# A two-layer attention and expert kernel: the first experts' second matmul as three rounded products, gates applied to finished sums, and sums and remainders moved to GpSimd

## What is computed

```python
def _L0_ffn_ref(x, Wg, W1, W2, W3):          # E=8 experts, F=256 hidden, top k=2
    scores = jnp.einsum('bsd,ed->bse', x, Wg)
    topk_scores, topk_idx = jax.lax.top_k(scores, k)
    topk_probs = jax.nn.softmax(topk_scores, axis=-1)
    h1 = jnp.einsum('bsd,efd->bsef', x, W1)
    h2 = jnp.einsum('bsd,efd->bsef', x, W2)
    hidden = jax.nn.silu(h1) * h2
    expert_out = jnp.einsum('bsef,edf->bsed', hidden, W3)
    onehot = jax.nn.one_hot(topk_idx, scores.shape[-1], dtype=x.dtype)
    gating = jnp.einsum('bsk,bske->bse', topk_probs, onehot)
    return jnp.einsum('bse,bsed->bsd', gating, expert_out)
```

## Time and profile before

| | |
|---|---|
| time, median of 3 runs | 1642.62 us |
| time of the profiled execution | 1642.04 us |
| its span | 1639.9 us |
| TensorE busy | 1490.6 us (91%) |
| VectorE busy | 1375.4 us (84%) |
| ScalarE busy | 1146.4 us (70%) |
| GpSimd busy | 167.9 us (10%) |

### The profile page before, as it was taken

How to read it: one execution, slowest core, us unless ns; L and a number is a source line. 1 busy time by engine, 2 the same in 40 slices (tenths; PEclk the granted TensorE clock), 3 DMA queues, 4 the chain that set the end, 5 groups by cost and what they waited for, 6 DMA issues and landing times.

```text
span 1639.9 us, 31494 instructions
## 1 busy us (share of the span) xinstructions
PE 1490.6 (91%) x11072; PEld 766.9 (47%) x11072; DVE 1375.4 (84%) x2375; ACT 1146.4 (70%) x1781; POOL 167.9 (10%) x231
## 2 busy tenths in 40 slices
PE   7998989599999999969999999999999998988996
PEld 4333333266556566623333333333333335766774
DVE  4899999668878678778999999999999963778776
ACT  4999999433332233217999999999999986766664
POOL 0000000101101001010000000000000001333332
PEclk9999999799999999967999999999999997999999
DMA  6635422221134322111111111111111111112111
GB/s 195 204 116 166 128 90 84 98 69 59 51 101 125 125 84 86 65 39 58 38 36 48 43 42 36 36 36 36 36 42 36 36 31 47 53 57 74 48 54 40
DMA packets 71022, 116.72 MB, mean 71 GB/s; under 512 B 23808, under 2 KB 33920, under 8 KB 70272
## 3 DMA queue, kind: packets, MB, share of 16 engines
q1 hardware_dynamic: 70912, 115.21, 23.1%
HBM read 73.49 MB, written 41.16 MB: 70 GB/s over the span
## 4 chain that ended last, share of the span: by engine, by line
PE 47%; DVE 21%; issue 12%; ACT 12%; DMA 4%; POOL 2%; SPq 2%; DVEq 0%; ACTq 0%; POOLq 0%
PE full_o L712 12%; PE max_pair L683 9%; ACT cprobs L485 7%; DVE negmax_h L801 7%; PE hid_pair L1021 7%; PE score L697 3%; PE causal_o L457 3%; PE bank L1114 3%; PE bank L1126 2%; DVE hid L1427 2%; PE triple L441 2%; DVE lin_u L1423 2%; DMA k_scr<-qk_hi 1%; DMA o_rcp<-rcp_scr 1%; SPq L960 1%
## 5 line engine op out<-in xcount | busy, mean ns | idle before, releaser
L765 ACT ACTIVATE probs<-score 128x512 f32<-128x512 f32 x1024 | 546.7, 597 | 84.3 <-PE score L697 64.3
L801 DVE TENSOR_REDUCE negmax_h<-max_pair 128x2 f32<-128x1024 f32 x512 | 587.4, 1215 | 19.6 <-PE max_pair L683 19.6
L712 PE MATMUL full_o<-probs,v_st 128*32 128x256 f32 x4096 | 331.0, 396 | 17.2 <-ACT o_sb L773 17.2
L697 PE MATMUL score<-q_st,k_st 32*128 32x512 f32 x1024 | 316.3, 501 | 4.2 <-ACT probs L765 4.2
L683 PE MATMUL max_pair<-k_st,q_st 32*128 32x512 f32 x1024 | 261.6, 510 | 11.4 <-DVE negmax_h L801 9.8
L485 ACT ACTIVATE cprobs<-triple 128x1536 f32<-128x1536 f32 x192 | 258.4, 1715 | 4.9 <-PE triple L441 4.9
L1223 ACT ACTIVATE act_s<-hid_pair 128x512 f32<-128x512 f32 x128 | 76.4, 597 | 193.8 <-PE hid_pair L1021 193.7
L683 PEld LDWEIGHTS max_pair<-k_st,q_st 32*128 32x128 f32 x1024 | 96.9, 187 | 231.9 <-DVE negmax_h L801 184.3
L1021 PE MATMUL hid_pair<-x_hi,w_hi 128*128 128x512 f32 x384 | 196.2, 511 | 0.0
L515 DVE TENSOR_SCALAR cprobs<-cprobs 128x1536 f32<-128x1536 f32 (+6 forms) x272 | 160.4, 617 | 3.2 <-ACT cprobs L485 3.1
L457 PE MATMUL causal_o<-cprobs,v_st 128*32 128x512 f32 (+3 forms) x1536 | 155.7, 501 | 2.2 <-DVE cprobs L515 2.2
(11 more groups left out here) (140 smaller groups left out, 1613.1 us busy)
## 6 DMA issues: line engine op xcount, KB each, us to landing
gate_all<-gate_scr SPq DMA_DIRECT2D x48, 512.0 KB, 4.9
o_scr<-o_sb SPq DMA_DIRECT2D x64, 256.0 KB, 2.1
k_st<-k_scr SPq DMA_DIRECT2D x64, 128.0 KB, 2.8
q_st<-q_scr SPq DMA_DIRECT2D x128, 64.0 KB, 2.5
k_st<-k_scr SPq DMA_DIRECT2D x64, 96.0 KB
q_st<-q_scr SPq DMA_DIRECT2D x64, 96.0 KB
q_scr<-qk_hi SPq DMA_DIRECT2D x18, 256.0 KB, 5.1
k_scr<-qk_hi SPq DMA_DIRECT2D x18, 256.0 KB, 4.7
```

The source lines that it names most:

```text
L697: nc.tensor.matmul(sbank[L.score_bank(e)][:, :], k_st[p][rows, kt * P:(kt + 1) * P], q_st[p][rows, q0:q0 + w], start=True, stop=True, tile ...
L712: last = nc.tensor.matmul(full_o[SLOT * j:SLOT * (j + 1), cols], v_st[p][:, kt, j, :], probs[s % NP][:, j, cols], start=(kt == 0 and part ...
L765: nc.scalar.activation(probs[s % NP][:, L.HEADS[j], :], sbank[L.score_bank(e)][:, :], ACT.Exp, scale=SCALE).then_inc(L.exp_done, 1)
L801: nc.vector.tensor_reduce(negmax_h[:, qt // TPC, half, heads[0]:heads[1] + 1:2, qt % TPC], ring[slot][:, :, :], AXX, ALU.max, negate=True) ...
```

## The change

Second layer: w3 is split into w3_hi (ScalarE, before the stage) and w3_lo (GpSimd, one 128x2048 subtraction), hid is split into hid_hi (ScalarE, act_upper) and a remainder (VectorE, dve_lower0), and the product is three rounded matmuls. Gates: VectorE multiplies h2 with silu(h1) directly, and the gate multiplies the finished sum of an expert, once every two steps (dve_weigh); GpSimd adds the eight results up (pool_add). Two PSUM banks alternate for the sums. Moved to GpSimd in the first experts: ot from chunk 1 on (pool_divide), the remainder of x (pool_x_lower), the remainders of q and k (pool_qk_lower) and the exponential of the gates (a power, in place of an Exp on ScalarE). Moved from VectorE to ScalarE: the copies into x_tm and v_all. TensorE now makes h1 and h2 three steps ahead instead of one, LATE is 2 instead of 0, and weigh, g_turn move from steps 7 and 9 to 8 and 10. SyncE's order stays, but its gate loads wait for the gated sums. At the end of the stage eight reductions instead of six lie beside the side work, in other places. In the last round of full attention the transpose, the router's hidden layer and the router each come one step earlier, GELU's table is loaded by an extra one-element activation, and the copies and remainders of the second experts' weights on VectorE come after x_turn. In the second experts GpSimd adds the last expert of a chunk before rstd of the next chunk instead of after it.

```diff
-LATE = (0, 2)
+LATE = (2, 2)
...
-    BESIDE_BACK = {6: (0, 1), 7: (2, 3), 8: (4, 5)}
+    BESIDE_BACK = {1: (0,), 2: (1,), 4: (2, 3), 7: (4,), 8: (5, 6), 9: (7,)}
...
+                    nc.scalar.activation(e_sm[:, 0, 0:1], mhalf[:, 0:1], ACT.Gelu)
...
-        for pl, steps in ((plan[0], (2, 4, 6, 7, 8, 9, 1, 1, 3, 4, None, 5, 7, 9)),
+        for pl, steps in ((plan[0], (2, 4, 6, 7, 8, 9, 1, 1, 3, 4, None, 5, 8, 10)),
...
-        EARLY = (3, 7, 9, 12)
+        EARLY = (3, 6, 8, 11)
...
-        RH_AT = 10
+        RH_AT = 8
...
-        h_banks, h_lead = [2, 4], [1, 3]
+        h_banks, h_lead = [2, 4], [3, 3]
...
+        lower = [[qk_hi[2], qk_hi[3], qk_lo[2], qk_lo[3]], hid_lo]
+        y_part = [o_sb[0], y_tmp]
...
-        def pe_product(pe, st, c, n):
-
-            pe.wait_ge(st.hid_ready, c * SPC + n + 1)
-            nc.tensor.matmul(bank[0][:, :], w3[:, n, :], hid[n % 2][:, :], start=(n == 0),
-                             stop=(n == SPC - 1)).then_inc(st.y_done, 1)
-
-        def pe_split_product(pe, st, c, n):
-
-            per = SPC // E1
+        def pe_product(pe, st, c, n, layer):
+
+            per = SPC // n_exp[layer]
             e, f = n // per, n % per
             if f == 0:
-                wait_used(pe, st.y_used, c * E1 + e - 1)
+                wait_used(pe, st.y_used, c * n_exp[layer] + e - 1)
             pe.wait_ge(st.hid_ready, c * SPC + n + 1)
-            hi, lo = hid_hi[n % HB], hid_lo[n % HB]
-            for a, (w, x) in enumerate(((w_hi[1], hi), (w_lo[1], hi), (w_hi[1], lo))):
-                last = nc.tensor.matmul(y_bank[e % 2], w[:, slice_of(n)], x[:, :], start=(f == 0 and a == 0),
+            hi, lo = hid_hi[n % HB][:, :], lower[layer][n % HB][:, :].bitcast(F32R)
+            if layer == 0:
+                up, down = w3_hi[:, n, :], w3_lo[:, n, :]
+            else:
+                up, down = w_hi[1][:, slice_of(n)], w_lo[1][:, slice_of(n)]
+            for a, (w, x) in enumerate(((up, hi), (down, hi), (up, lo))):
+                last = nc.tensor.matmul(y_bank[e % 2], w, x, start=(f == 0 and a == 0),
                                         stop=(f == per - 1 and a == 2))
             last.then_inc(st.y_done, 1)
...
+                if layer == 0 and n == pl.norm2:
+                    act.wait_ge(st.norm2, back + 1)
+                    nc.scalar.activation(x_tm[:, bass.ds(back * TPC, TPC), :], x_out[:, :, :],
+                                         ACT.Copy).then_inc(st.x_kept, 1)
...
+                if layer == 0 and n == pl.v:
+                    act.wait_ge(st.v_ready, back + 1)
+                    nc.scalar.activation(v_all[:, bass.ds(back * TPC, TPC), :],
+                                         bank[2][:, :].rearrange("p (t c) -> p t c", c=D),
+                                         ACT.Copy).then_inc(st.v_saved, 1)
...
-                if layer == 0 and n == pl.router + 1:
-                    act.wait_ge(st.gate_pre, front + 1)
-                    nc.scalar.activation(p12[:, 1, :], lead[:, :], ACT.Exp).then_inc(st.gate_exp, 1)
...
+        def act_upper(act, st, m):
+
+            act.wait_ge(st.m_done, NS + m + 1)
+            wait_used(act, st.y_done, m - HB + 1)
+            nc.scalar.activation(hid_hi[m % HB][:, :], hid[m % 2][:, :], ACT.Copy).then_inc(st.hi_done, 1)
...
+                    act.wait_ge(st.m_done, c * SPC + n + 1)
                     nc.scalar.activation(act_s[n % 2][:, :], hbank[n % 2], ACT.Silu).then_inc(st.s_done, 1)
+                    if c + n > 0:
+                        act_upper(act, st, c * SPC + n - 1)
...
-                act.wait_ge(st.y_done, (c + 1) * SPC)
-                nc.scalar.activation(y_sb[:, :], bank[0][:, :], ACT.Copy).then_inc(st.y_saved, 1)
...
+        def dve_weigh(dve, st, c, e, layer):
+
+            n_e = n_exp[layer]
             dve.wait_ge(st.gate_in[e // 2], 16 * (c + 1))
-            dve.wait_ge(st.y_done, c * SPC + (e + 1) * (SPC // E1))
+            dve.wait_ge(st.y_done, c * SPC + (e + 1) * (SPC // n_e))
             if e == 0:
                 wait_used(dve, st.y_turned, c)
             elif e > 1:
-                dve.wait_ge(st.y_sum, 2 * c + e - 1)
-            nc.vector.scalar_tensor_tensor((y_sb if e == 0 else y_tmp)[:, :], y_bank[e % 2], be2[:, e:e + 1],
-                                           gate_all[e // 2][:, e % 2, :], ALU.add, ALU.mult).then_inc(st.y_used, 1)
+                dve.wait_ge(st.y_sum, (n_e - 2) * c + e - 1)
+            to = (y_sb if e == 0 else y_part[layer])[:, :]
+            gate = gate_all[e // 2][:, e % 2, :]
+            if layer == 0:
+                nc.vector.tensor_tensor(to, y_bank[e % 2], gate, ALU.mult).then_inc(st.y_used, 1)
+            else:
+                nc.vector.scalar_tensor_tensor(to, y_bank[e % 2], be2[:, e:e + 1], gate, ALU.add,
+                                               ALU.mult).then_inc(st.y_used, 1)
+
+        def dve_lower0(dve, st, m):
+
+            dve.wait_ge(st.hi_done, m + 1)
+            wait_used(dve, st.y_done, m - HB + 1)
+            nc.vector.tensor_tensor(lower[0][m % HB][:, :].bitcast(F32R), hid[m % 2][:, :],
+                                    hid_hi[m % HB][:, :].bitcast(F32), ALU.subtract).then_inc(st.hid_ready, 1)
+
         def dve_chunk(dve, st, c, par, back, front, layer):
             per = SPC // n_exp[layer]
             for n in range(SPC):
                 e = n // per
                 if layer == 0:
-                    if e % 2 == 0 and n % per == 0:
-                        dve.wait_ge(st.gate_in[e // 2], 16 * (c + 1))
-                    wait_used(dve, st.y_done, c * SPC + n - 1)
-                    dve.wait_ge(st.h_ready, c * SPC + n + 1)
-                    nc.vector.tensor_tensor(lin_u[n % 2][:, :], hbank[2 + n % 2], gate_all[e // 2][:, e % 2, :],
-                                            ALU.mult).then_inc(st.u_done, 1)
-                    dve.wait_ge(st.u_done, NS + c * SPC + n + 1)
-                    dve.wait_ge(st.s_done, h_banks[layer] + c * SPC + n + 1)
-                    nc.vector.tensor_tensor(hid[n % 2][:, :], act_s[n % 2][:, :], lin_u[n % 2][:, :],
-                                            ALU.mult).then_inc(st.hid_ready, 1)
+                    m = c * SPC + n
+                    dve.wait_ge(st.s_done, h_banks[0] + m + 1)
+                    wait_used(dve, st.hid_ready, m - 1)
+                    nc.vector.tensor_tensor(hid[n % 2][:, :], hbank[2 + n % 2], act_s[n % 2][:, :],
+                                            ALU.mult).then_inc(st.m_done, 1)
+                    if m > 0:
+                        dve_lower0(dve, st, m - 1)
...
+                if layer == 0 and n % 2 == 0 and (n > 2 or back is not None):
+                    dve_weigh(dve, st, c if n > 2 else back, (n // 2 - 2) % E0, 0)
...
+            pool_rstd(pool, pc, st.stats, st.rstd, 0, 1)
+            pool.wait_ge(st.w3_upper, 1)
+            nc.gpsimd.tensor_tensor(w3_lo[:, :, :], w3[:, :, :], w3_hi[:, :, :].bitcast(F32),
+                                    ALU.subtract).then_inc(st.w3_lower, 1)
+            pool_gate_exp0(pool, st, 0)
+            for c in range(2 * B + 1):
+                front = c + 1 < 2 * B
+                if front:
+                    pool_divide(pool, st, c + 1)
+                if c > 0:
+                    pool_add(pool, st, c - 1, E0 - 2, 0)
+                    pool_add(pool, st, c - 1, E0 - 1, 0)
+                if front:
+                    pool_rstd(pool, pc, st.stats, st.rstd, 0, c + 2)
+                if c == 2 * B:
                     pool_fill_values(pool, layers[1])
-                pool_back(pool, pc, st, c, 0)
+                if c > 0:
+                    pool_rstd(pool, pc, st.stats2, st.rstd2, 1, c)
+                if front:
+                    pool_x_lower(pool, st, c + 1)
+                if c < 2 * B:
+                    pool_add(pool, st, c, 1, 0)
+                if front:
+                    pool_gate_exp0(pool, st, c + 1)
+                if c < 2 * B:
+                    pool_add(pool, st, c, 2, 0)
+                if c > 0:
+                    for a in range(2):
+                        pool_rot(pool, st, c - 1, a)
+                if c < 2 * B:
+                    pool_add(pool, st, c, 3, 0)
+                if c > 0:
+                    for a in range(2):
+                        pool_qk_lower(pool, st, c - 1, a)
+                if c < 2 * B:
+                    pool_add(pool, st, c, 4, 0)
+                    pool_add(pool, st, c, 5, 0)
...
+                if c > 0:
+                    pool_add(pool, st, c - 1, E1 - 1, 1)
+                if front:
                     pool_rstd(pool, pc, st.stats, st.rstd, 0, c + 2)
                 if c > 0:
-                    pool_add(pool, st, c - 1, E1 - 1)
-                    pool_back(pool, pc, st, c - 1, 1)
+                    pool_rstd(pool, pc, st.stats2, st.rstd2, 1, c)
                 if c < 2 * B:
-                    pool_add(pool, st, c, 1)
```

(7 more changed lines are left out.)

128 lines of the change are left out of this document (65 added, 63 removed).

## The result

The changed kernel takes 1650.0 us (median of 20 runs, 1645.1 to 1664.7), the kernel before 1642.0 (median of 20). The ratio is 1.0052, 95% interval 1.0036 to 1.0068: slower by half a per cent, where the forecast was 1640, a little faster than before. 1650 lies inside the stated range of 1608 to 1661, but on the other side of no change. The profiled execution has a span of 1645.9 us against 1639.9, so the trace holds 6.0 of the 8 us.

A forecast was written before the change was run, and what follows sets the result against it. The loop gate write, load landing, next gate write was taken to bound the first experts. Terms -5 + 28 - 8 - 2 - 3 - 12 = -2 on 1642.04 gave 1640 us, range 1608 to 1661.

The forecast's parts named there:

- the start: First experts up to the second gate write: cheaper steps against the added w3_lo subtraction, -5 us (-8 to +3).
- the end of the stage with the last round: End of first experts -2 us (-5 to +2); last full-attention round -3 (-7 to 0), ScalarE's 2.69 us gap going.
- the second experts: Last expert's addition before rstd removes six TensorE waits, 10.2 us, plus 3.5 for clock: -12 us (-17 to -4).
- way from load to gate write: First experts, from the next chunk's inputs landing to the following gate write: grows from 30.5 to 36.1 us.
- L: The landing of the load of the next chunk's inputs (o_rcp) in the first experts.
- G to L: First experts, from gate write to landing of the next chunk's inputs: stays at 17.3 us.
- the term of +28: First experts, five turns from gate write to gate write, each 5.6 us longer: +28 us (-5 to +45).
- Gate 7: VectorE's gate of expert 7 waits for GpSimd's sum behind the division, until L+3.4; VectorE's next steps stand behind it.
- rival A: First experts: hand-overs close, x_turn and router don't wait, turns 1 us shorter than before; 1607 us, chance 0.25.
- end of the stage: -8: First experts, last gate write to last product: 56.9 us before, 49 after, -8 us (-10 to -3).
- rival C: Second experts gain nothing because another wait (VectorE's remainder, ScalarE) takes the place; 1652 us, chance 0.11.
- Rival B: First experts: GpSimd's additions hold VectorE 0.6 us each, 4.2 a turn, 21 in all; 1661 us, chance 0.22.

The follow-up runs named there:

- e1: Changed kernel with SyncE's load of o_raw and o_rcp ahead of the stores of split q and k in the first experts: 1620.3 us, ratio 0.9869.
- e5: Kernel before, with SyncE's load of o_raw and o_rcp moved ahead of the stores as in e1: 1638.4 us, ratio 0.9982.
- e7: Changed kernel with GpSimd's additions of experts 6 and 7 ahead of the division into ot instead of behind it: 1651.9 us, ratio 1.0062.
- e2: Changed kernel with GpSimd's order in the second experts put back, rstd of the next chunk before the last expert's addition: 1660.1 us, ratio 1.0112.
- e3: Changed kernel with the last round of full attention, and the second experts' weight copies and remainders, as in the kernel before: 1651.3 us, ratio 1.0050.
- e4: Changed kernel with GpSimd's 128x2048 subtraction for w3_lo after the first gates' power instead of before it: 1652.0 us, ratio 1.0061.
- e12: e1 with the w3_lo subtraction cut into four of 128x512, one before the first gates' power, three behind the division: 1632.7 us, ratio 0.9932.
- e6: Changed kernel with GpSimd's seven additions per chunk of the first experts 4 columns wide instead of 512: 1648.1 us, ratio 1.0040.
- e10: e1 with side step norm at 2 instead of 3, SyncE's load started before waiting for gates, and VectorE's reciprocal four steps sooner: 1621.6 us, ratio 0.9873.
- e14: e10 with ScalarE's copy of x_out into x_tm behind its copies xt and x_hi instead of ahead: 1621.5 us, ratio 0.9883.
- e13: e1 with ten extra rounded matmuls on TensorE before its wait for xs, every chunk but the first: 1627.1 us, ratio 0.9912.

## Why the prediction was wrong

The loss in the loop was forecast and came. The step that failed is the one that set gains against it: the start (-5), the end of the stage with the last round (-5) and the second experts (-12) were put at -22 together and gave -7.8 in the trace. In each of them the time of a wait or of matmuls that go was taken for time of the kernel, and nothing was charged for what is late next. That turned a forecast of 2 us less into 6 us more.

**What bounds the kernel: right for the kernel after, overstated for before.** The loop over SyncE sets the changed kernel's first experts (e1: 30 us from taking the load ahead). The kernel before was only level with it (e5: 4 us at the median, between 0 and 6).

**The way from load to gate write: right, nearly step by step.** In the turn shown, from L = 416.3: statistics of res done at L+7.2 (forecast 7.5), xs at L+13.3 (13.7), x_out at 15.5 (15.9), best two at 20.9 (21.4), x2_turn at 21.4 (21.8), gate write at 35.4 (36.1). G to L took 17.6 us (forecast 17.3), and the load was issued 13.3 to 14.9 us behind the gate write. One reading of the walk is off: TensorE, at half clock behind its wait for ot, reached x_turn at L+12.0 and not L+10.3, and stood 1.3 us there instead of 3.4. But the term of +28 was made from the growth of one turn of 47.9 us and then added to five that took 48.8 on average. The walk's own turn, 17.3 + 36.1 = 53.4, less 48.8 gives +23; +21.7 was measured. The step that read 5.6 from a typical turn mis-sized it by about 5.

**Gate 7 behind the sum: a wait of VectorE, not a link of the loop.** The walk had all of VectorE's next steps behind it, and the argument against rival A named it; e7 took it away and a turn went from 53.2 to 52.9. Rival A didn't come true all the same, and its gain isn't to be had by moving the load alone: with the load out of the way a turn takes 47.5 us with the new second layer (e1) and 47.5 with the old (e5). TensorE is busy 43.4 us in a turn of e1 and 45.4 in one of e5, at a granted clock of 0.96 and 1.00; the 2.7 us that sixteen cheaper products save go into its wait for xs, 3.1 us a turn, and into the clock behind it. They come through only at the end of the stage: -8 forecast, -7.8 measured. The term's own parts make 47.9 us there and not 49, so it should have read -9.

**The second experts: the step that failed.** The term was -12, measured -6.8 (e2: 7.0 in the trace). Its 10.2 for the waits removed was right and its 3.5 for the clock nearly (TensorE's wait for y_sb fell from 13.5 in the earlier trace rows to 3.3, its busy time from 229.7 in the earlier trace rows to 226.7). What failed is that nothing was charged for what is late next: 4.0 more for remainders (14.2 before) and 3.7 for the statistics. About half of what rival C described came true. (With 0.4 taken off six times the term's parts make -11.3, which was written as -12.)

**The last round: -3 forecast, nothing measured (e3).** The gap that was to go went, and ScalarE's waits for scores stayed the same in sum; the reordered round ran at a lower granted clock (0.82 against 0.85). Together with the end of stage, where -2 was forecast, the stretch gave +0.6. Full attention lies in this stretch and differs by up to 11 us from trace to trace, so this number is loose by some us; for the end of stage alone no run shows a value.

**The start: -5 forecast, -1.6 measured.** The first hidden matmul is at 318.7 in both kernels. From the second gate write to the third a turn takes 47.4 us (351.38 to 398.73), before 47.7 (352.65 to 400.33): 0.3 saved, where sixteen steps at 0.17 make 2.7. So here too the cheaper products didn't come through. The subtraction for w3_lo held xs for 4 us, where the walk had let it run beside w_lo; but e4 and e12 moved it and the first gate write came no more than 0.5 us earlier, so it doesn't explain the missing 3.4. The rest stays open.

**Rival B.** Its mean was met (114.9 us in 128 remainders, 0.90); its price wasn't: e6 narrowed the additions and gained 2 us. The Trainium skill, SBUF — State Buffer, section Who interferes with whom, says that a tensor_tensor with both inputs in SBUF contends with GpSimd's reads. The traces agree as to the operation: remainders, with both inputs in SBUF, were held, and none of the 128 multiplications into hid, which read PSUM, took over 0.69 us. The row that the prediction named for the second half of this, rot at 537.15, shows nothing, since it ended at 537.83 and the addition began at 537.91. And B's sentence that the kernel is slower than before from 2 us a turn on doesn't fit the sum: with -2 in all, 0.4 us a turn is enough.

So the sum failed by its small gains, 22 us forecast and 8 found, and not by its large loss. With +22 in place of +28 and the rest as forecast it would have been 1634, further off: the error in the loop hid a part of the others.

## What to carry to other kernels

Before counting an engine's saved time, find the loop of hand-overs that repeats once a chunk, transfers included, and look for the one call in it that doesn't need to stand there: here the order of two calls was worth 30 us in the changed kernel, more than the 22 us of matmul time that 128 products save at 0.17 each, and 4 in the kernel before, where that loop was level with others. Remove a wait and charge what is late next at once; in the second experts 7.4 of 14 us came back, and along one engine's chain nearly all. A term that is a difference is to be taken from the same mean on both sides.

The best kernel of the study is e1, with e10 and e14 level, at 1620.3 us, 1.3% under the kernel before (0.9843 to 0.9896) and 1.8% under the changed one.

## What the runs showed of the hardware

- GpSimd's 128x2048 subtraction took 4.49 us, about 3.6 times one of 128x512 (1.26), and held VectorE's operation beside it for its length: one of the four 128x128 pieces of xs took 4.51 us instead of 0.33 (changed kernel), and one operation on 128x4 4.49 instead of 0.16 (e4).
- Behind stalls of 3 us TensorE's granted clock was at half for about 3 us in one kernel (e1) and 10 in one turn of another with the same order (e12); with matmuls in the stall it was 0.99 instead of 0.96 over five turns (e13).
- Full attention took 667.9 us with a granted clock of 0.80 in its first 100 us (e12), 669.1 with 0.78 (before), 673.1 with 0.73 (e1), 676.4 with 0.66 (e5) and 679.4 with 0.64 (e4).
